# Adding the step size on TensorE inside a selective scan, in place of an addition on VectorE and a product on GpSimd

## The reference

```python
xz = einsum('bld,kd->blk', xn, W_x)          # xn: layer norm of x
dt_raw, b_ssm, c_ssm = split(xz, [128, 144])
dt = softplus(einsum('blr,dr->bld', dt_raw, W_dt) + b_dt)
d_a = exp(dt[..., None] * -exp(A_log))
dbx = dt[..., None] * b_ssm[:, :, None, :] * xn[..., None]
# over time: h = d_a * h + dbx;  y = sum_n(h * c)
```

## Time and profile before

| | us |
|---|---|
| median of 3 runs | 3053.68 |
| lowest and highest run | 3049.96, 3054.82 |
| the profiled execution: span from first to last instruction | 3057.4 |
| PE busy over the span | 2742.0 |
| DVE busy | 1789.4 |
| POOL busy | 1529.0 |
| ACT busy | 1298.1 |

### The profile page before, as it was taken

How to read it: one execution, slowest core, us unless ns; L and a number is a source line. 1 busy time by engine, 2 the same in 40 slices (tenths; PEclk the granted TensorE clock), 3 DMA queues, 4 the chain that set the end, 5 groups by cost and what they waited for, 6 DMA issues and landing times.

```text
span 3057.4 us, 37567 instructions
## 1 busy us (share of the span) xinstructions
PE 2742.0 (90%) x13484; PEld 1445.2 (47%) x13484; DVE 1789.4 (59%) x3787; ACT 1298.1 (42%) x2689; POOL 1529.0 (50%) x944
## 2 busy tenths in 40 slices
PE   4668889898998879988868999999899999999998
PEld 2455555555555534333325555555544444444443
DVE  5899999999999742222236666665624444222222
ACT  4557576675866411110107666766722220111111
POOL 6999999999999702212125555555500001121211
PEclk7769999998998989989979999999999999999999
DMA  5344544545545479999960000000225323999997
GB/s 194 141 167 153 195 172 161 192 155 182 180 167 174 141 273 352 340 336 341 336 201 1 29 29 29 29 29 15 89 87 181 121 86 130 312 334 336 342 348 219
DMA packets 198955, 557.76 MB, mean 182 GB/s; under 512 B 24880, under 2 KB 26800, under 8 KB 198256
## 3 DMA queue, kind: packets, MB, share of 16 engines
q1 hardware_dynamic: 180624, 513.27, 48.7%
q0 software_dynamic: 17088, 40.90, 5.8%
q10 hardware_dynamic: 1056, 1.18, 0.1%
HBM read 479.50 MB, written 75.79 MB: 182 GB/s over the span
## 4 chain that ended last, share of the span: by engine, by line
PE 54%; DVE 3%; ACT 2%; POOL 2%; issue 2%; DMA 1%; POOLq 0%; SPq 0%; DVEq 0%; ACTq 0%
PE bank L1133 11%; PE bank L1159 5%; PE bank L1036 5%; PE bank L1057 5%; PE bank L1071 5%; PE bank L1184 5%; PE bank L1241 4%; PE bank L1218 3%; PE bank L1206 2%; PE bank L1230 2%; POOL arena L1940 2%; PE bank L1116 1%; PE bank L1172 1%; ACT arena L1763 1%; PE bank L1043 1%
## 5 line engine op out<-in xcount | busy, mean ns | idle before, releaser
L1844 POOL TENSOR_TENSOR arena<-arena 128x1024 f32<-128x1024 f32 x256 | 607.5, 2373 | 7.9 <-PE bank L986 5.0
L1692 ACT ACTIVATE bank<-arena 128x512 f32<-128x512 f32 x512 | 346.6, 689 | 317.6 <-DVE arena L1330 198.5
L986 PE MATMUL bank<-arena 128*128 128x128 f32 x2048 | 306.3, 303 | 146.1 <-POOL arena L1850 145.8
L1940 POOL TENSOR_TENSOR arena<-arena 128x2048 f32<-128x2048 f32 (+3 forms) x128 | 296.9, 2323 | 276.4 <-DVE arena L1560 276.3
L986 PEld LDWEIGHTS bank<-arena 128*128 128x128 f32 x2048 | 260.4, 156 | 231.7 <-POOL arena L1850 186.2
L1763 ACT ACTIVATE arena<-arena 128x256 f32<-128x256 f32 (+3 forms) x512 | 287.3, 566 | 148.8 <-DVE arena L1551 125.2
L1133 PE MATMUL bank<-arena 128*64 128x352 f32 x2048 | 343.1, 491 | 0.0
L1850 POOL TENSOR_TENSOR arena<-arena 128x512 f32<-128x512 f32 x256 | 333.8, 1304 | 17.5 <-DVE arena L1330 17.5
L1330 DVE TENSOR_TENSOR_SCAN arena<-bank,arena 128x512 f32<-128x512 f32 x256 | 310.7, 1214 | 26.5 <-POOL arena L1844 19.4
L1330 DVE TENSOR_TENSOR_SCAN bank<-bank,arena 128x512 f32<-128x512 f32 x256 | 308.4, 1205 | 0.0
L1057 PE MATMUL bank<-arena 128*128 128x512 f32 x640 | 288.3, 593 | 7.6 <-ACT arena L1719 7.6
(11 more groups left out here) (145 smaller groups left out, 4159.0 us busy)
## 6 DMA issues: line engine op xcount, KB each, us to landing
arena<-scratch_bc SPq DMA_DIRECT2D x128, 1024.0 KB, 5.4
arena<-in_w_gate SPq DMA_DIRECT2D x128, 704.0 KB
arena<-in_w_up SPq DMA_DIRECT2D x128, 704.0 KB
arena<-in_w_down SPq DMA_DIRECT2D x128, 512.0 KB
arena<-in_w_down SPq DMA_DIRECT2D x128, 192.0 KB
scratch_x<-arena SPq DMA_DIRECT2D x16, 1024.0 KB, 4.5
scratch_xn<-arena SPq DMA_DIRECT2D x15, 1024.0 KB, 4.1
arena<-scratch_x SPq DMA_DIRECT2D x44, 256.0 KB, 6.0
```

The source lines that it names most:

```text
L986: i = nc.tensor.matmul(y[:, t * P:(t + 1) * P], w[:, n, t * P:(t + 1) * P], p.ident, is_transpose=True, start=False, stop=g == GROUPS - 1 ...
L1692: nc.scalar.activation(bank[p.da_bank(k, n)][:, :], block_of(p.dt, b, c), ACT.Exp, scale=p.alog[:, c, state:state + 1]).then_inc(*p.decaye ...
L1844: nc.gpsimd.tensor_tensor(out=p.hb[k % HB], in0=over(block_of(p.dtx, b, c), 1, NG), in1=p.bc[k // 2 % NBC][:, 0], op=ALU.mult).then_inc(*p ...
L1940: nc.gpsimd.tensor_tensor(out=own, in0=own, in1=over(p.rden[:, k % 2, :], 2, width), op=ALU.mult).then_inc(*p.divided.up(k))
```

## The change

`dt_sum` on VectorE and `dtx` on GpSimd (both for a half of two blocks) are taken out. For every block c there are now three operations: `dsum` on TensorE, two matmuls with the identity that add the dt tile and the soft tile in a bank of the ring; `dt_copy` on ScalarE, which copies the bank into the dt tile; and `dtx` on VectorE, which multiplies the bank by the turned block xn and writes the dtx tile. The product waits for the copy as well, so that the two don't read the bank at the same time, and it is what frees the bank. `decay` waits for the copy of its own block, `feed` for the product of its block. `dsum` becomes a product of the three-bank ring, at steps 27, 28, 30 and 31, and the two takers follow one step behind, at 28, 29, 31 and 32.

```diff
-SOFT = (("soft_exp", (24, 28)), ("soft_ln", (26, 29)), ("dt_sum", (27, 30)), ("dtx", (28, 31)))
+SOFT = (("soft_exp", (24, 28)), ("soft_ln", (26, 29)))
+DSUM, DSUM_LAG = (27, 28, 30, 31), 1
-FIRST_DT, FIRST_SOFT = (0, 0), (("soft_exp", 3), ("soft_ln", 4), ("dt_sum", 5), ("dtx", 6))
+FIRST_DT, FIRST_SOFT, FIRST_DSUM = (0, 0), (("soft_exp", 3), ("soft_ln", 4)), (5, 6)
...
 def prepare_track(b):
+        yield DSUM[c], ("dsum", b, c)
+        yield DSUM[c] + DSUM_LAG, ("dt_copy", b, c)
+        yield DSUM[c] + DSUM_LAG, ("dtx", b, c)
...
-TAKERS = ("turned", "dtr_out", "bc_out", "dt_out", "logit", "folded", "silu", "hid", "so")
+TAKERS = ("turned", "dtr_out", "bc_out", "dt_out", "dt_copy", "dtx", "logit", "folded", "silu", "hid", "so")
...
+    def dt_sum(b, c):
+        ring = p.rings[0]
+        out = bank[ring.bank("dsum", b, c)]
+        PE.wait_bank(ring, "dsum", b, c)
+        PE.wait_ge(p.soft_ln, b, c // 2)
+        nc.tensor.matmul(out[:, :], p.ident, block_of(p.dt, b, c), start=True, stop=False)
+        nc.tensor.matmul(out[:, :], p.ident, block_of(p.dtx, b, c), start=False, stop=True).then_inc(
+            *ring.made.up("dsum", b, c))
...
-    def dt_sum(b, h):
-        V.wait_ge(p.soft_ln, b, h)
-        dt, soft = half_of(p.dt, b, h), half_of(p.dtx, b, h)
-        nc.vector.tensor_tensor(out=dt, in0=dt, in1=soft, op=ALU.add).then_inc(*p.dt_ready.up(b, h))
+    def dtx(b, c):
+        ring = p.rings[0]
+        V.wait_ge(ring.made, "dsum", b, c)
+        V.wait_ge(p.dt_ready, b, c)
+        nc.vector.tensor_tensor(out=block_of(p.dtx, b, c), in0=bank[ring.bank("dsum", b, c)][:, :],
+                                in1=p.s_xnT[b % 2][:, c, :], op=ALU.mult).then_inc(
+                                    *ring.taken_by["dve"].up("dsum", b, c))
...
+    def dt_copy(b, c):
+        ring = p.rings[0]
+        A.wait_ge(ring.made, "dsum", b, c)
+        nc.scalar.copy(block_of(p.dt, b, c), bank[ring.bank("dsum", b, c)][:, :]).then_inc(*p.dt_ready.up(b, c))
...
-    def dtx(b, h):
-        xnT = p.s_xnT[b % 2][:, h * (HC // 2):(h + 1) * (HC // 2), :]
-        G.wait_ge(p.dt_ready, b, h)
-        nc.gpsimd.tensor_tensor(out=half_of(p.dtx, b, h), in0=half_of(p.dt, b, h), in1=xnT,
-                                op=ALU.mult).then_inc(*p.dtx_ready.up(b, h))
...
     def feed(k):
-        G.wait_ge(p.dtx_ready, b, c // 2)
+        G.wait_ge(p.rings[0].taken_by["dve"], "dsum", b, c)
```

More of the change, by code:

```diff
@@ L282, in first_track @@
         yield FIRST_DT[c - 2] + DT_LAG, ("dt_out", 0, c)
+        yield FIRST_DSUM[c - 2], ("dsum", 0, c)
+        yield FIRST_DSUM[c - 2] + DSUM_LAG, ("dt_copy", 0, c)
+        yield FIRST_DSUM[c - 2] + DSUM_LAG, ("dtx", 0, c)
     for name, at in FIRST_SOFT:
@@ L318, in first_steps @@
     plan += [("dt", 0, 0), ("dt", 0, 1), ("dt_out", 0, 0), ("dt_out", 0, 1)]
-    plan += [("soft_exp", 0, 0), ("soft_ln", 0, 0), ("dt_sum", 0, 0), ("dtx", 0, 0)]
+    plan += [("soft_exp", 0, 0), ("soft_ln", 0, 0)]
+    for c in range(2):
+        plan += [("dsum", 0, c), ("dt_copy", 0, c), ("dtx", 0, c)]
     plan += [("x_in", 1), ("ff_w", 0), ("pads", 0)] + [("feed", k) for k in range(AHEAD)]
     return plan
-TAKERS = ("turned", "dtr_out", "bc_out", "dt_out", "logit", "folded", "silu", "hid", "so")
+TAKERS = ("turned", "dtr_out", "bc_out", "dt_out", "dt_copy", "dtx", "logit", "folded", "silu", "hid", "so")
 def scan_plan():
@@ L766, in semaphores @@
         sig = self.counter
-        made_by = {"turn": "turn", "bc": "bc", "dtr": "dtr", "dt": "dt", "gate": "gate", "gate_wide": "gate_wide", "sg": "sg", "su": "su",
+        made_by = {"turn": "turn", "bc": "bc", "dtr": "dtr", "dt": "dt", "dsum": "dsum", "gate": "gate", "gate_wide": "gate_wide", "sg": "sg", "su": "su",
                    "sd": "sd", "fold": "fold", "merge": "merge", "lists": "lists", "xturn": "xturn", "down": "down",
@@ L771, in semaphores @@
         taken_by = {"turned": ("turn", "act"), "bc_out": ("bc", "act"), "dtr_out": ("dtr", "act"),
-                    "dt_out": ("dt", "act"), "logit": ("gate", "act"), "wide_out": ("gate_wide", "act"), "silu": ("sg", "act"), "hid": ("su", "dve"),
+                    "dt_out": ("dt", "act"), "dtx": ("dsum", "dve"), "logit": ("gate", "act"), "wide_out": ("gate_wide", "act"), "silu": ("sg", "act"), "hid": ("su", "dve"),
                     "so": ("sd", "dve"), "folded": ("fold", "dve"), "merge": ("merge", "dve"), "lists": ("lists", "dve"),
@@ L807, in semaphores @@
         self.soft_exp, self.soft_ln = sig("soft_exp", "soft_exp"), sig("soft_ln", "soft_ln")
-        self.dt_ready, self.dtx_ready = sig("dt_ready", "dt_sum"), sig("dtx_ready", "dtx")
+        self.dt_ready = sig("dt_ready", "dt_copy")
         self.bc_in = [sig(f"bc_in{r}", "bc_in", by=16, where=lambda n, r=r: n % NBC == r) for r in range(NBC)]
@@ L1243, in attn_out @@
         i.then_inc(*ring.made.up("wo", b, t))
-    work = {"constants": constants, "barrier": barrier, "turn": turn, "bc": bc, "dtr": dtr, "dt": dt, "sum": y_sum,
+    work = {"constants": constants, "barrier": barrier, "turn": turn, "bc": bc, "dtr": dtr, "dt": dt, "dsum": dt_sum, "sum": y_sum,
             "gate": gate, "gate_wide": gate_wide, "sg": shared_gate, "su": shared_up, "sd": shared_down, "fold": fold, "merge": merge,
@@ L1581, in vector_engine @@
     work = {"constants": constants, "barrier": barrier, "stats": stats, "stats_a": stats_a, "apply": apply, "decay_w": decay_w,
-            "dt_sum": dt_sum, "scan": scan, "x1": x1, "hid": hidden, "so": shared_out,
+            "dtx": dtx, "scan": scan, "x1": x1, "hid": hidden, "so": shared_out,
             "route_max": route_max, "route1": route1, "masks": masks, "folded": folded, "pick": pick, "merge": merge, "lists": lists,
@@ L1683, in decay @@
         A.wait_ge(p.decay_set)
-        A.wait_ge(p.dt_ready, b, c // 2)
+        A.wait_ge(p.dt_ready, b, c)
         for n in range(NG):
@@ L1788, in scalar_engine @@
             "route1": route1, "turned": turned, "bc_out": bc_out, "dtr_out": dtr_out,
-            "dt_out": dt_out, "soft_exp": soft_exp, "soft_ln": soft_ln, "decay_w": decay_w, "scan": decay,
+            "dt_out": dt_out, "soft_exp": soft_exp, "soft_ln": soft_ln, "dt_copy": dt_copy, "decay_w": decay_w, "scan": decay,
             "logit": logit, "wide_out": wide_out, "silu": silu, "route_exp": route_exp, "up": expert_gate, "flip": flipped, "scale": scale,
@@ L1941, in divide @@
                                 op=ALU.mult).then_inc(*p.divided.up(k))
-    work = {"constants": constants, "barrier": barrier, "sums": sums, "rstd": rstd, "dtx": dtx, "feed": feed, "weigh_c": weigh_c, "route_w": route_w,
+    work = {"constants": constants, "barrier": barrier, "sums": sums, "rstd": rstd, "feed": feed, "weigh_c": weigh_c, "route_w": route_w,
             "so": shared_sum, "turnover": turnover, "gather": gather, "give": give,
```

## The result

| | before | changed |
|---|---|---|
| median of the runs, us | 3053.65 | 3116.97 |
| lowest and highest, us | 3049.96, 3054.82 | 3113.77, 3118.16 |
| profiled execution, span, us | 3057.4 | 3112.0 |
| PE, DVE, ACT, POOL busy, us | 2742.0, 1789.4, 1298.1, 1529.0 | 2801.2, 1764.4, 1313.7, 1484.1 |

One run of the changed kernel was disturbed (8469.94 us) and is left out of the median and the ratio (with it, the median of four is 3117.56). The ratio is 1.0198 (95%: 1.0176 to 1.0221), so the change costs some 60 us; the two medians lie 63 apart. That is slower, as forecast, inside the range of 3042 to 3126, and 24 us above the forecast of 3093. It is also above the range that the prediction gave to its own case A (3075 to 3110) and inside that of rival C (3110 to 3135), so the time alone doesn't tell which of the two mechanisms came; the trace has to.

The account below looks back on a forecast made before the run. No engine alone bounds the scan stage: DVE and POOL have two to four us of air per batch, PE roughly 15. Terms 44.2 - 8 + 10 - 4 = +42, rounded to +39, gave 3093 us, range 3042 to 3126.

Parts of the forecast that it names:

- case A: Scan stage: ScalarE stops for dsum 2 and dsum 3 behind PE's queue; 3093 us, own range 3075 to 3110, chance 0.60.
- rival C: Scan stage: PE's clock stays low through sg 4 too, x1 waits for the y_sum behind it; +66, 3120 us, chance 0.17.
- the prediction's own clock: Reckoned timeline of batch 3 from step 26 at 516.2; step 34 begins at 562.8, not 555.5, a loss of 7.3 us.
- One of its signs: In front of the scans: DVE's idle grows from under 20 to 70 us or more, released by ACT.
- Steps 26 to 34 of batches 1 to 6: Stops for dsum 2 and dsum 3 lengthen these stretches, +44.2 us over six batches before the clock term.
- one step of the argument: Batch 3: scan 33 begins at 556.2 after ACT's copy 3, load and decay; step 33 then takes 6.5 us as before.
- DVE keeps pace: Batch 3: without dt_sum (5.28 us) DVE is 3.7 us early at step 31.
- The clock: PE's 4.5 us idle before dsum 3 drops its clock; dsum 3 takes 3.4 us, copy 3 comes 1.7 later, +10 us.
- Batch 0: No shared products, POOL sets the pace: -8.7 in steps 26 to 34, -2.4 for early dtx, 3 given back, -8 us.
- Elsewhere in the scan: With POOL ahead, DVE's other two-input SBUF instructions wait less: -0.7 per batch, -4 us, between 0 and -15.
- Prologue: Before the first scan: dt_sum 1.22 and dtx 2.36 against dsum 1.9, copy 0.6, product 0.7; nothing within 1 us.
- Rival B: Scan stage: the two waits don't arise and the relief of DVE and POOL counts; about -28, 3026 us, chance 0.16.

Follow-up runs that it names:

- experiment 9: The kernel before with the change made only for the second half of batch 0 and both halves of batch 1: 3045.62 us, 0.9959 against the kernel before.
- experiment 3: The changed kernel with one matmul for each sum, the soft part not added: 3104.56 us, 1.0148 against the kernel before, two runs only.
- experiment 4: The kernel before with dt_sum and dtx cut to 8 of 512 columns, nothing added elsewhere: 3037.20 us, 0.9927 against the kernel before.
- Experiment 1: The changed kernel with copy and product two steps behind their sum in place of one: 3084.70 us, 1.0093 against the kernel before.
- Experiment 2: The changed kernel with the sums of blocks 2 and 3 at steps 34 and 36, not 30 and 31: 3061.98 us, 1.0015 against the kernel before.

## Why the prediction was right in kind and too small in size

**The mechanism held**: ScalarE stopped before copy 2 and copy 3, dsum 3 was held by silu 3, and batch 0 alone gained. On the prediction's own clock, moved by the 14.0 us by which step 26 of batch 3 came later, copy 2 was due to end at 561.2 and ended at 561.1, and silu 3 was due to end at 565.7 and ended at 565.6. The prediction also wrote 5.2 us for the first stop, su 3 and dsum 2 alone; by its own clock it was 8.0 (538.4 to 546.4), as sg 3 was still to do, and it measured 6.78. One of its signs failed: VectorE's idle in front of the scans, behind ScalarE, was to grow to 70 us or more and came to 29.6. The time shows up in front of dtx (30.8, released by the copy) and x1 (33.3, released by y_sum) instead.

**Steps 26 to 34 of batches 1 to 6**: forecast +44.2 and +10 for the clock, measured +68.5. Odd batches were to take 46.6 + 1.7 = 48.3 us and took 51.8, 50.2 and 49.9; even ones 46.2, and took 48.3, 48.3 and 48.9. The 14 us between come from one step of the argument: "ACT: copy 3 554.2, table load and first decay 556.2. There scan 33 begins. The 6.5 us of step 33 follow". Two things were missing. First, scan 33 isn't released by ScalarE but by VectorE's own queue: x1 waits for the y_sum behind the late dsum 3 (4.28 us), then hid and dtx come, and the scan starts at 572.78, where the forecast with its 1.7 us for the clock had 571.9. Second, step 33 took 7.7 us in place of 6.5: in batch 3 the next x1 waits 1.09 us for PE. In all six batches step 33 is 1.2 us longer than before, which is 7 of the 14; the rest is read from batch 3 alone. The prediction had x1 waiting for the y_sum under rival C and didn't put it in the sum. I also left out a table load, that of the decays behind soft_ln (547.78, 1.28 us), so silu 2 ended at 553.7, not at 552.4; PE had slack for it there, as dsum 2 came no later than forecast. Nor did "DVE keeps pace" hold in full: at step 31 it was 2.2 us early, not 3.7, as it waited 1.8 us for decays in each of steps 28 and 29. That changed nothing behind it.

**The clock** was priced right for dsum 3: the fall came (0.50 in the row above), and dsum 3 took 3.6 us in place of 1.72, +1.9 for the 1.7 assumed. The y_sum behind it, for which x1 waits, ran slower too, 1.69 us where the one before the stop took 1.04; the sum had nothing for that. The clock didn't stay low: from 571 to 576 us, where sg 4 runs, it is 1.00, and the means of the six stretches are 0.93 to 0.96. So rival C's clock part failed, while its second half, x1 behind the y_sum, happened. The Trainium skill (TensorE: Matmul & The Clock Gate, "HAM oscillation — how this bites in real kernels") has idle gaps of PE send its clock down, and the trace agrees with 0.50 behind a gap of 4.33 us. The prediction says that its sum would be 10 us lower without that rule; it wouldn't, as the earlier trace rows alone carry the term.

**Batch 0** (steps 2 to 34): forecast -8, and -11 with the 3 us by which the sum was rounded down for it; measured -12.0, of it -6.3 in steps 26 to 34 and -5.7 in 2 to 12, where I had counted -2.4 for the early dtx and nothing for the early dt_sum (no run takes the two apart). The 3 us given back for a low clock weren't due, since PE's clock there was 0.86 and not 0.59.

**Elsewhere in the scan**: forecast -4, measured about -2 as the rest of the sum (60.4 - 5.7 + 12.0 - 68.5). That this is near is luck. The term stood for VectorE's other additions and products with two SBUF inputs waiting less, and the rest holds one that did the opposite, a product of the routing in step 13 of batch 6:

```profile
899.94 6.42 DVE L1420 TENSOR_TENSOR arena<-arena 128x256 f32<-128x256 f32 x1
```

Its shortest takes 0.43 us. It made that step 5.9 us longer than before, while in the kernel before the longest one (4.15 us) stood in batch 5. In the trace of experiment 9 a 6.42 stands in batch 4, which is made the old way. So a single trace can hold some 6 us of this that the change didn't make.

**Prologue**: forecast nothing, measured +5.7 (first scan at 42.15 for 36.44). Here the price of a dsum was wrong. PE had been idle and ran at its low level, and both sums stand in front of the first decay. TensorE, then ScalarE:

```profile
33.45 2.04 PE L986 MATMUL bank<-arena 128*128 128x512 f32 x2 [5.20 <-ACT arena L1696]
35.28 1.91 PE L987 MATMUL bank<-arena 128*128 128x512 f32 x2
...
37.23 0.58 ACT L1701 COPY arena<-bank 128x512 f32<-128x512 f32 x1 [3.93 <-PE bank L987]
39.46 0.58 ACT L1701 COPY arena<-bank 128x512 f32<-128x512 f32 x1 [1.64 <-PE bank L987]
```

From the end of soft_ln to the first scan it is 42.15 - 33.31 = 8.8 us, where it was 6.1. That is 2.7 of the 5.7; the other 3 lie before the first sum, where the two programs are the same, and no run shows their cause. In the profiles here the first scan starts between 40.0 and 42.2 us where the prologue has the full sums, at 37.3 with half of them (experiment 3), and between 34.8 and 38.7 with the old pair.

**Rival B** (faster, 3026) failed by its condition, no stop at the copies. Its size isn't shown either: with the old pair cut and nothing put in its place (experiment 4) the gain was 22 us, with the additions still waiting, where B had 28 with the new work in.

**What stays open**: how the loss divides between the order of ScalarE's queue and PE's own backlog. Experiment 1 leaves PE's order as it is and moves the takers alone; it gives back some 32 us of 61, but PE's stop before dsum 3 goes with it. Experiment 2 gives back some 24 more, and moves sums and takers together. That sums placed one by one in gaps of PE's queue could pay in batches 1 to 6 wasn't tried.

## What to carry to other kernels

An operation handed to an engine with an order of its own can cost more by its place in that queue and in the bank ring than by its duration: here 59 us more of busy time on PE, on average within its air, and 38 us of takers made 60 us of loss at one place and 5 at another. Before moving one, write down the queue with the instruction ahead of it and the one behind it, on every engine that takes part, and look at the busiest single steps, not at the mean air of a batch. And a change that loses on the whole can still pay in the stretch whose engines are free; there alone it made this kernel 0.4% faster.

## What I hadn't expected of the hardware

In these traces a VectorE addition with both inputs in SBUF waits not only for one instruction of GpSimd but can wait for a whole run of them: 7.62 us for 16 columns, through the running feed and four further instructions (experiment 4), 8.65 for the full one, whose shortest took 1.22, and 6.42 for a product of 256 columns, whose shortest took 0.43. The products of a PSUM bank with an SBUF tile beside the same GpSimd work, 30 of the new dtx, took 684 ns each:

```profile
L1340 DVE TENSOR_TENSOR arena<-bank,arena 128x512 f32<-128x512 f32 x30 | 20.5, 684 | 30.8 <-ACT arena L1701 30.8
```

The Trainium skill (SBUF — State Buffer, "Who interferes with whom") says that a VectorE instruction with two SBUF inputs contends with a GpSimd instruction that reads SBUF, and that the shared port pair is an exclusive lock. The traces agree that such an instruction is held up beside GpSimd's (7.62 us) and the products of a bank aren't (684 ns), and they show a wait longer than one instruction.
